# Four attention layers on one core: the eight-head loop written out, rows of the maximum issued by SyncE, keys and queries projected from group 0

## The reference

```python
def layer(x, heads):                       # x: [8, 128, 1024]
    h = group_norm(x, 32) * gamma + beta
    q, k, v = wq @ h + bq, wk @ h + bk, wv @ h + bv
    # layers 0 and 1: 8 heads of 16 channels; layers 2 and 3: 1 head of 128
    w = softmax(scale * q^T k)             # [1024, 1024] for each head
    return x + wp @ (v w^T) + bp
```

## Time and profile before

| | us |
|---|---|
| median of 3 runs | 2429.26 |
| lowest, highest | 2421.52, 2431.30 |
| profiled execution | 2425.72 |
| span in its profile | 2424.0 |
| first exponential to the end of image 15 (`many_heads`) | 85.9 to 1842.1 |
| busy: PE, DVE, ACT | 2199.5, 1729.6, 1652.4 |

### The profile page before, as it was taken

The page is one execution under the profiler, slowest core; times in us unless marked ns, Lnnn a source line. Parts: engine busy times, 40 slices in busy tenths (PEclk is TensorE's granted clock), DMA queues, the critical chain, the costliest instruction groups (busy, mean ns, idle before and its releaser), DMA issues. The chain is left out here.

```text
span 2424.0 us, 32992 instructions
## 1 busy us (share of the span) xinstructions
PE 2199.5 (91%) x11778; PEld 1059.9 (44%) x11778; DVE 1729.6 (71%) x2115; ACT 1652.4 (68%) x3009; POOL 458.5 (19%) x682
## 2 busy tenths in 40 slices
PE   1899999989998998999899989999997999999999
PEld 0333333333333333333333333333333888888887
DVE  0887778767786877677677767777743777777776
ACT  0376666656666666676566656676765888888887
POOL 4102011111202020111112020201102333333331
PEclk7699999979899998999799989999986999999999
DMA  7235160515244260505153342516101111111111
GB/s 143 28 50 71 39 96 21 89 29 77 43 63 64 43 99 21 87 22 87 31 75 53 53 62 44 86 34 91 25 16 50 62 52 45 63 54 42 61 50 46
DMA packets 63660, 137.36 MB, mean 57 GB/s; under 512 B 14880, under 2 KB 26272, under 8 KB 63392
## 3 DMA queue, kind: packets, MB, share of 16 engines
q1 hardware_dynamic: 60064, 133.90, 30.2%
q10 hardware_dynamic: 3456, 1.57, 0.4%
HBM read 57.31 MB, written 22.02 MB: 33 GB/s over the span
## 5 line engine op out<-in xcount | busy, mean ns | idle before, releaser
L473 DVE TENSOR_REDUCE h_half_nmax<-h_s_ps 128x2 f32<-128x1024 f32 x1024 | 1209.1, 1220 | 423.0 <-PE h_s_ps L660 419.5
L591 ACT ACTIVATE h_probs<-h_st_ps 128x512 f32<-128x512 f32 x2048 | 1078.0, 601 | 564.3 <-PE h_st_ps L764 461.8
L764 PE MATMUL h_st_ps<-h_qrep,h_krep 51*128 51x512 f32 x2048 | 694.3, 507 | 65.4 <-ACT h_probs L591 41.0
L764 PEld LDWEIGHTS h_st_ps<-h_qrep,h_krep 51*128 51x128 f32 x2048 | 289.4, 194 | 759.0 <-ACT h_probs L591 578.5
L650 PE MATMUL h_pv<-h_probs,h_vT 128*32 128x512 f32 x4096 | 585.2, 645 | 26.4 <-ACTq L595 25.2
L660 PE MATMUL h_s_ps<-h_krep,h_qrep 48*128 48x512 f32 x2048 | 414.0, 445 | 44.9 <-SPq L241 30.6
L660 PEld LDWEIGHTS h_s_ps<-h_krep,h_qrep 48*128 48x128 f32 x2048 | 216.8, 199 | 150.2 <-DVE h_half_nmax L473 90.9
L1288 PE MATMUL o_s<-o_k,o_q 128*128 128x512 f32 x768 | 224.4, 428 | 8.7 <-DVE o_q L1109 5.7
L366 POOL TENSOR_SCALAR h_nparts<-h_nmax 128x16 bf16<-128x16 f32 x64 | 16.3, 254 | 1092.3 <-DVE h_nmax L480 1092.3
L1288 PE MATMUL o_pv<-o_pT,o_vT 128*128 128x512 f32 x768 | 208.1, 406 | 0.8 <-ACTq L1215 0.8
L1103 DVE TENSOR_TENSOR o_pT<-o_t,o_pT 128x512 fp32r<-128x512 f32 x256 | 164.5, 685 | 46.2 <-ACT o_pT L1240 43.7
(11 more groups left out here) (106 smaller groups left out, 1189.6 us busy)
## 6 DMA issues: line engine op xcount, KB each, us to landing
h_krep<-h_kp SPq DMA_DIRECT2D x96, 256.0 KB, 9.2
h_qrep<-h_qp SPq DMA_DIRECT2D x192, 128.0 KB, 14.1
x_res<-out_dram SPq DMA_DIRECT2D x32, 512.0 KB, 3.3
num<-av SPq DMA_DIRECT2D x128, 64.0 KB
rrep<-rden_dram SPq DMA_DIRECT2D x16, 512.0 KB
out_dram<-o_y SPq DMA_DIRECT2D x16, 512.0 KB
h_x_in<-out_dram SPq DMA_DIRECT2D x15, 512.0 KB, 3.3
out_dram<-h_y SPq DMA_DIRECT2D x15, 512.0 KB, 2.6
```

The costliest lines, as they stand in the source:

```text
L473: reduce = nc.vector.tensor_reduce(half_nmax[:, c, th, :, pair % MP], s_ps[slot][:, :, :], AX.X, ALU.max, negate=True)
L591: nc.scalar.activation(probs[g % 2][:, j, :], st_ps[n % COLUMN_BANKS][:, :], ACT.Exp, scale=1.0 / CH ** 0.5).then_inc(columns_done, 1)
L764: nc.tensor.matmul(st_ps[n % COLUMN_BANKS][:, :], krep[par][part, quad * 2 + m, st * P:(st + 1) * P], qrep[par][part, th, quad * 2 + m, :] ...
```

## The change

- **Loop.** On all five engines `Fori` is replaced by a Python loop over the 8 pairs, so the program of `many_heads` is written out in full. The counting down of semaphores at the end of each pair stays.
- **Rows of the maximum.** ScalarE only copies to `mrow` and signals `mrow_ready`; SyncE issues the DMAs, four smaller ones in place of two, since `nparts` and `qrep` have another layout. They stand in SyncE's queue at four fixed places of an image.
- **`qrep`** is `[P, 4, T]` instead of `[P, 2, 4, HALF]`, so the queries are replicated with 6 DMAs instead of 12.
- **Places.** K0, K1, Q0, Q1 stand at k = 0, 2, 3, 4 instead of 3, 4, 6, 7; the average at k = 14 of the odd step (group 30) of the image before instead of group 0, for the first image ahead of the loop. `invert` stands at k = 6 instead of 5. GpSimd makes the coefficients at the end of an image and splits the keys before the maximum.
- **Input.** The copy of `x` to `out` at the start is gone; layer 0 reads `x`.

```diff
-    AVG, K0, K1, MAX1, Q0, Q1, V, MAX0, O = 0, 3, 4, 5, 6, 7, 8, 13, 14
+    K0, K1, Q0, Q1, MAX1, V, MAX0, O = 0, 2, 3, 4, 5, 8, 13, 14
+    AVG = 14
...
-                if s % 2 == 0 and k in (AVG, V, O):
+                if k in (V, O) if s % 2 == 0 else k == AVG and not (last and s == 3):
                     rows[s, k, "other"] = len(rows)
...
-        qrep = [sb(f"qrep{i}", [P, 2, HEADS // 2, HALF], F32R) for i in range(2)]
+        qrep = [sb(f"qrep{i}", [P, HEADS // 2, T], F32R) for i in range(2)]
...
+                for which, of, n, order in (("k", krep[par], 1, (0, 0, 1)), ("q", qrep[par], 2, (0, 1, 0))):
+                    sp.wait_ge(parts_ready, 2 * u + n)
+                    for term, part in enumerate(order):
+                        for r in range(2):
+                            to = r * ROWS + term * CH
+                            sp.dma_start(of[to:to + CH, :, :].bitcast(F32),
+                                         parts[which][r * ROWS:(r + 1) * ROWS, part, :].bitcast(F32)).then_inc(rep_dma, 16)
...
+            def max_rows(n, par, quad, th):
+
+                sp.wait_ge(mrow_ready, n)
+                for r in range(2):
+                    for m in range(2):
+                        of = (r * 2 + m) * MAX_PARTS * MP // 2
+                        sp.dma_start(qrep[par][r * ROWS + KS:r * ROWS + KM, quad * 2 + m, th * HALF:(th + 1) * HALF].bitcast(F32),
+                                     mrow[th][of:of + MAX_PARTS * MP // 2, :].bitcast(F32)).then_inc(mrow_dma, 16)
+
+            def image(n):
+
+                return x[n, :, :] if n < B else out[n % B, :, :]
...
-            for b in range(B):
-                sp.dma_start(out[b, :, :], x[b, :, :]).then_inc(copy_dma, 16)
             sp.wait_ge(ones, 1)
             replicate(0, 0)
...
-                        last_output(out[(i + B - 1) % B, :, :])
+                        last_output(image(i - 1))
                         sp.wait_ge(rden_ready, u + 1)
                         spread()
+                    max_rows(4 * u + 1, u, 0, 1)
                     if not (last and u == 1):
                         replicate(1 - u, u)
+                    max_rows(4 * u + 2, u, 1, 0)
 
                     sp.wait_ge(y_ready, 2 * (u + 1))
...
                     kept["gather"](sp, 0, av_dma)
+                    max_rows(4 * u + 3, u, 1, 1)
+                    if not (last and u == 1):
+                        max_rows(4 * u + 4, 1 - u, 0, 0)
...
             def body(first=False, last=False):
                 for u in range(2):
-                    coefficients(u)
-                    split_max(4 * u + 1, 1)
                     if not (last and u == 1):
                         pool.wait_ge(parts_free, u + 1)
                         split(2 * u + 1, "k")
+                    split_max(4 * u + 1, 1)
+                    if not (last and u == 1):
                         split(2 * u + 2, "q")
...
                     if not (last and u == 1):
                         split_max(4 * u + 4, 0)
-                pool.sem_inc(coef_ready, -2)
+                        coefficients(u)
...
-                        if s % 2 == 0 and k == 5:
+                        if s % 2 == 0 and k == 6:
...
-            def max_rows(n, bank, step, th):
+            def max_rows(n, bank, th):
 
                 act.wait_ge(columns_ready, n)
                 own.done(nc.scalar.copy(mrow[th][:, :], st_ps[bank][:, :].bitcast(BF16)[0:MAX_PARTS * MH, 0:P]))
                 act.sem_inc(columns_done, 1)
-                par, quad = step // 2 % 2, step % 2
-                for r in range(2):
-                    act.dma_start(qrep[par][r * ROWS + KS:r * ROWS + KM, th, quad * 2:(quad + 1) * 2, :].bitcast(F32),
-                                  mrow[th][r * MAX_PARTS * MP:(r + 1) * MAX_PARTS * MP, :].bitcast(F32)).then_inc(mrow_dma, 16)
+                act.sem_inc(mrow_ready, 1)
...
+            pe.wait_ge(stats_ready, 2)
+            pe.wait_ge(rows_done, 2 * LEAD + 1)
+            average(0)
...
-            pe.wait_ge(rows_done, 2 * LEAD)
-            pe.sem_inc(rows_done, -2 * LEAD)
+            pe.wait_ge(rows_done, 2 * LEAD + 3)
+            pe.sem_inc(rows_done, -(2 * LEAD + 1))
...
-                            pe.wait_ge(mrow_dma, 32 * (2 * s + k // TILES + 1))
+                            pe.wait_ge(mrow_dma, 64 * (2 * s + k // TILES + 1))
...
-            body(first=True)
-            with pe.Fori(1, PAIRS - 1):
-                body()
-            body(last=True)
+            for pair in range(PAIRS):
+                body(pair == 0, pair == PAIRS - 1)
```

More of the change, by code:

```diff
@@ L171, in many_heads @@
         idle = sb("idle", [P, 2])
-        nparts = [sb(f"nparts{i}", [P, 2, MAX_PARTS, MP], BF16) for i in range(2)]
+        nparts = [sb(f"nparts{i}", [P, 2, 2, MAX_PARTS, MP // 2], BF16) for i in range(2)]
         mrow = [sb(f"mrow{i}", [MAX_PARTS * MH, P], F32R) for i in range(2)]
@@ L200, in many_heads @@
         nparts_ready = sem("nparts_ready")
+        mrow_ready = sem("mrow_ready")
         mrow_dma = sem("mrow_dma")
@@ L209, in many_heads @@
         g_in = sem("g_in")
-        rep_dma, load_dma, av_dma, den_dma, copy_dma, store_dma = (
-            sem(n) for n in ("rep_dma", "load_dma", "av_dma", "den_dma", "copy_dma", "store_dma"))
+        rep_dma, load_dma, av_dma, den_dma, store_dma = (
+            sem(n) for n in ("rep_dma", "load_dma", "av_dma", "den_dma", "store_dma"))
         act_own, dve_own, pool_own = sem("act_own"), sem("dve_own"), sem("pool_own")
@@ L308, in body @@
                     else:
-                        load_g(out[(i + 2) % B, :, :], (i + 2) // B, NW if last else NG)
+                        load_g(image(i + 2), (i + 2) // B, NW if last else NG)
                     sp.dma_start(wo[:, :], w[i // B, :, W_P:W_P + NO]).then_inc(load_dma, 16)
@@ L320, in body @@
                 sp.sem_inc(y_ready, -4)
-            body(0, first=True)
-            with sp.Fori(1, PAIRS - 1) as pair:
-                body(pair)
-            body(PAIRS - 1, last=True)
+            for pair in range(PAIRS):
+                body(pair, pair == 0, pair == PAIRS - 1)
             sp.wait_ge(av_dma, 16 * (QUAD + 1))
@@ L381, in _ @@
             pool.sem_inc(nmax_ready, -1)
+            coefficients(1)
+            pool.sem_inc(coef_ready, -2)
             own.drain()
@@ L405, in body @@
                 own.drain()
-            body(first=True)
-            with pool.Fori(1, PAIRS - 1):
-                body()
-            body(last=True)
+            for pair in range(PAIRS):
+                body(pair == 0, pair == PAIRS - 1)
         @block.vector
@@ L520, in body @@
                             n = order[s, k, "other"]
-                            if k == AVG:
-                                coefficients(n + 1, n % ROW_SLOTS, *((NEXT_EPS, True) if last and u == 1 else ()))
+                            if s % 2 == 1:
+                                coefficients(n + 1, n % ROW_SLOTS, *((NEXT_EPS, True) if last else ()))
                             elif k == V:
@@ L531, in body @@
                 own.drain()
-            body(first=True)
-            with dve.Fori(1, PAIRS - 1):
-                body()
-            body(last=True)
+            for pair in range(PAIRS):
+                body(pair == 0, pair == PAIRS - 1)
         @block.scalar
@@ L601, in body @@
                             if k == MAX1:
-                                max_rows(n + 1, bank, s, 1)
+                                max_rows(n + 1, bank, 1)
                             elif k == MAX0:
-                                max_rows(n + 1, bank, s + 1, 0)
+                                max_rows(n + 1, bank, 0)
                             else:
@@ L610, in body @@
                 own.drain()
-            body(first=True)
-            with act.Fori(1, PAIRS - 1):
-                body()
-            body(last=True)
+            for pair in range(PAIRS):
+                body(pair == 0, pair == PAIRS - 1)
             act.wait_ge(pv_done, 2)
@@ L732, in for_dve @@
                         pe.wait_ge(rows_done, n + 1)
-                        if k == AVG:
+                        if s % 2 == 1:
                             pe.wait_ge(stats_ready, u + 1)
-                            if last and u == 1:
+                            if last:
                                 combine_weights(nc, s_ps[slot][:, 0, :], wg)
```

43 lines of the change are left out of this document (17 added, 26 removed).

## The result

| | before | after |
|---|---|---|
| median of runs on one chip, us | 2429.99 | 2547.31 (2543.49 to 2553.74) |
| ratio to before | | 1.0493, 95% interval 1.0458 to 1.0528 |
| profiled execution / its span, us | 2425.72 / 2424.0 | 2550.63 / 2548.9 |
| busy PE, DVE, ACT, us | 2199.5, 1729.6, 1652.4 | 2191.9, 1729.4, 1659.0 |
| images 1 to 14 in `many_heads`, us | 1534.8 | 1644.2 |

A forecast was written before the change was run, and what follows sets the result against it. It took TensorE's order and waits as the bound. Fourteen images +24.8, pair ends +9.3, start +2.7, image 0 +1.5, image 15 +4.8 gave +43.1 on 2425.7: 2469 us, range 2415 to 2545.

The forecast's parts named there:

- The loop: Pair ends: written-out code has no jump stall, but each end still costs 1.33 us, +9.3 us over seven.
- rival 4: Pair ends: the stall stays, from fetching rather than jumping, 7 x 4.0 us more and clock; 2497 us or more, chance 0.08.
- ScalarE without the issues: ScalarE no longer issues the maximum's DMAs: 0.82 us gained for each of four maxima in an image.
- The first wait: k = 8: TensorE waits 8.6 us in images 1 to 15 for rows queued on SyncE behind reciprocal and spread.
- The clock behind it: After the k = 8 wait: low granted clock costs 2.5 us in k = 8 and 0.9 in k = 9, 3.4 in all.
- Rival 2: After the k = 8 wait: clock stays low for k = 8 and four more groups, 8.4 us; 2544 us, chance 0.20.
- The two meet: k = 16: rows land at 64.6 us, TensorE arrives at 64.8, so a short or no wait.
- Second half: From k = 16 to the image's end: 46.3 us, with two maxima cheaper and the average added at k = 30.
- The ends: Outside images 1 to 14: start +2.7 us, image 0 +1.5, image 15 +4.8, removing the input copy 0.
- Rival 1: SyncE's queue costs nothing: rows arrive before k = 8 and k = 16, image 99.4 us; total 2286 us, chance 0.11.
- Rival 3: Everything hidden that can be; the second wait rules with 64.6, image 109.4 us; total 2431 us, no change, chance 0.13.

The follow-up runs named there:

- loop_only: The kernel before with only its `Fori` loop written out as a Python loop over the pairs; 2367.97 us, ratio 0.9737 to before.
- sync_rows_k4_avg12: sync_rows_k4 with the average at k = 12 of the odd step in place of 14; 2305.00 us, ratio 0.9524 to before.
- scalar_rows_k4_avg12: rows_undone with the reciprocal at k = 4 instead of 6 and the average at k = 12 instead of 14; 2377.73 us, ratio 0.9810 to before.
- rows_inside: Changed kernel with SyncE issuing the rows of k = 13 ahead of its wait for the replication's landing; 2473.08 us, ratio 1.0201 to before.
- sync_rows_k4: Changed kernel: reciprocal at k = 4, SyncE issues k = 5 rows before the spread wait, k = 13 rows before the replication wait; 2317.31 us, ratio 0.9518.
- rows_undone: Changed kernel with the maximum's rows issued by ScalarE again, old `qrep` and `nparts` layouts, twelve query transfers; 2490.48 us, ratio 1.0299 to before.
- loop_recip_k6: loop_only with VectorE's reciprocal at k = 6 in place of k = 5; 2432.40 us, ratio 1.0044 to before.

## Why the prediction was wrong

The direction was right and the time was not: 2551 in the profiled execution against 2469, and 2 us above the range's upper end by the median. The sum's steps, one by one:

- **The loop.** Right: no stall is left, and rival 4 falls. A pair's end costs 1.2 us in loop_only, near the 1.33 that I took, but in the changed kernel only 2.7 - 2.3 = 0.4 (last groups of images 7 and 8), so 6.5 us of my 9.3 did not come. loop_only shows the whole part: -65 us.
- **ScalarE without the issues.** Right in kind: 0.82 taken for each maximum. In image 9 of the changed kernel the groups 21 and 22 take 5.76 us (1221.27 to 1227.03), where the earlier trace rows had 6.56 for the same two: 0.80 gained. Whole images at full clock say much the same: image 9 takes 100.84 us in sync_rows_k4_avg12 and 104.52 in scalar_rows_k4_avg12, 3.7 for four maxima. The exponential behind the maximum's copy now comes after 0.25 us of idle time, where the earlier trace rows had 1.71.
- **The first wait.** Right: 9.73 measured and 8.6 forecast. The reciprocal came 1.3 us after the start of group 6, where I had put it at the start. From there to the first issue it took 8.97 us (forecast 9.04), and from the first issue to TensorE's release 4.3, issues and landing together, against 4.5.
- **The clock behind it.** Right in sum: k = 8 takes 8.7 in place of 5.2, +3.5, against 3.4, but all of it falls in k = 8 and none in k = 9. Rival 2, whose time of 2544 is close to the measured one, had the wrong mechanism: the clock is 1.00 from k = 9 on.
- **"The two meet" at k = 16. This step failed.** I had TensorE there at 64.8 and the rows at 64.6. Measured in image 9: TensorE at 66.2, the rows at 67.9. The path to TensorE was right: 30.9 us from the release at k = 8, as forecast. The chain on SyncE was late by small amounts of one sign, 3.3 us in all: reciprocal 1.65, four issues 0.6, replication 1.3, against 0.2 gained at the end. I had taken 1.4 us off the replication for its longer pieces, and it took 29.5 us as before. Two numbers that differ by 0.2 us, each summed from five terms, are not a tie but an open question, and I gave the outcome "a short wait" no price. Its price is not its length: rows_inside shows 4.8 us an image, 74 us in all, for waits of 2.2 us in the mean, and 2473 us without them against my 2469.
- **Second half.** 46.4 in rows_inside against 46.3. The fall of the clock behind the second wait makes it 48.3. It is counted from the first exponential of k = 16, and 64.8 was the time of TensorE's product: the 0.6 us between the two (1206.02 to 1206.62) was missing from my sum.
- **The ends.** Start +4.4 against 2.7: the replication ahead of it was not shorter. Image 0 +5.8 against 1.5: it has only the second wait, 4.6 us there, and the fall. Image 15 +5.4 against 4.8. Copy 0, as forecast.

The difference of 81.8 us between 2550.6 and 2468.8 is then: fourteen images +75.3 (of it the second wait 14 x 4.76 = 66.6, a first half longer by about 1.4 each, 19.6, with those 0.6 in it, less the pair ends, 6.5, and less the 0.3 for clock falls that I had added, 4.2), start +1.7, image 0 +4.3, image 15 +0.6. The parts agree with the whole within 0.3 us.

**Rival 1** (the queue costs nothing, 2286) failed as stated, and its rule with it: moving the issue did not only save ScalarE's time. But the 2286 was the price of an order without the waits, and sync_rows_k4 comes within 12 us of it in its profiled execution (2297.3).

**Rival 3** had the second wait set the image, with the rows at 64.6. They do set it, at 67.9: the mechanism was there, and its 2431 was too low by the same late chain and the clock.

**What I did not see at all** is what rows_undone found. I took the wait at k = 16 for a matter of SyncE's program order alone. Order is a part of it, since rows_inside takes the wait away by order. But rows issued early on another queue still land only when the 16 DMA engines are nearly through with the replication, and the kernel before obeys that too. The earlier trace rows had the replication end near 1124.6 and k = 16 in the same place; I read that as slack of TensorE and not as its release. The reciprocal's move, which I counted only towards the first wait, is therefore one of the two large losses. By mean image, in this order of steps and from one profiled execution each: loop -4.5, reciprocal at k = 6 +5.0 (loop_recip_k6), the other places +3.1 (rows_undone, which contains them all), rows on SyncE where the change put them +4.3. The average at k = 14 in place of 12 accounts for 3.8 us an image in the pair of kernels where it was moved alone; how much of the +3.1 is its move from group 0 was not tried.

## What to carry to other kernels

A transfer that is issued early from an idle queue is not early if a large one is in flight on the same DMA engines: it lands behind it. Find in the trace what the last landing before each wait really hung on, and start that chain sooner; here one reciprocal two groups earlier, and rows issued inside waits that stood there anyway, turned +4.9% into -5%. Where two chains meet within a microsecond or two, price the short wait with the clock fall behind it, since that was the larger part here.

## What the chip showed that I had not expected

- ScalarE's two transfers of 12 KB, issued by 1152.6 us, had no packet served before 1161 while 631 packets of SyncE's queue were; then all 54 went within four microseconds. Issued ahead of the replication, two such transfers went at once.
- Longer pieces in the replication changed nothing: 990 packets of SyncE's queue and 91% of the 16 engines' time over 30 us, against 1440 packets and 96% over 29 us. It is 3.2 MB at 106 to 111 GB/s either way. The DMA view of the changed kernel, 1172 to 1202, and of before, 1095 to 1124:

```profile
DMA packets 991, 3.18 MB, mean 106 GB/s; under 512 B 198, under 2 KB 222, under 8 KB 990
...
q1 hardware_dynamic: 990, 3.16, 91.1%
```

```profile
DMA packets 1497, 3.21 MB, mean 111 GB/s; under 512 B 294, under 2 KB 342, under 8 KB 1494
...
q1 hardware_dynamic: 1440, 3.15, 96.3%
```

- The granted clock fell to 1.2 GHz in images where TensorE never waited over 1.1 us. With the average at k = 14 the low stretches were longer than with it at k = 12, which cost 3.8 us in an image of 109; the maximum is its neighbour either way.
